# State-space stage of a fused decoder: B and C rows in rings of their own, the scan in place in SBUF, the product issued one step ahead

## The reference

```python
xn = (x - mu) * rsqrt(var + eps) * ln_w + ln_b
x_in, z = split(xn @ W_in)
xc = silu(causal_conv4(x_in) + conv_b)
dt_r, Bm, Cm = split(xc @ W_xproj)          # 8, 16 and 16 columns
dt = softplus(dt_r @ W_dt + b_dt)
def step(h, inp):                           # over the 128 tokens
    dA = exp(dt_t[:, :, None] * A)
    h = h * dA + dt_t[:, :, None] * B_t[:, None, :] * u_t[:, :, None]
    y = einsum('bdn,bn->bd', h, C_t)
y = (ys + xc * D_param) * silu(z)
out = x + y @ W_out                         # then a layer norm
```

## Time and profile before

| | us |
|---|---|
| median of 3 runs (lowest, highest) | 1881.98 (1881.71, 1882.33) |
| the profiled execution | 1878.54 |
| its span, first to last instruction | 1876.7 |
| first product of the state-space steps starts | 711.64 |
| last hC of POOL starts | 1239.76 |

### The profile page before, as it was taken

One profiled execution on the slowest core, in us unless ns is written; L12 is line 12 of the kernel. 1 busy time (PEld: TensorE's weight loads), 2 busy tenths in 40 slices (PEclk: granted clock), 3 DMA queues, 4 the chain that ended last, 5 costly groups with the idle time before them and its releaser, 6 DMA issues. The chain is left out here.

```text
span 1876.7 us, 29075 instructions
## 1 busy us (share of the span) xinstructions
PE 1478.6 (79%) x9959; PEld 992.7 (53%) x9963; DVE 1427.8 (76%) x2651; ACT 875.9 (47%) x1347; POOL 905.7 (48%) x794
## 2 busy tenths in 40 slices
PE   8989987999699986886877777658988831399991
PEld 4555545988466652332323323226767621399990
DVE  6999995879478868889888888967777757744445
ACT  3545543576544455665555645325666511022224
POOL 4446441444400116787677677654443200177653
PEclk8999998999899998998988888999999965599995
DMA  5000000000000013454444454420000050277765
GB/s 147 2 0 0 0 1 21 8 1 2 12 1 0 0 47 93 122 139 106 134 131 119 121 135 127 137 95 35 5 9 5 2 152 0 65 265 238 238 187 141
DMA packets 84090, 142.82 MB, mean 76 GB/s; under 512 B 11050, under 2 KB 36818, under 8 KB 83458
## 3 DMA queue, kind: packets, MB, share of 16 engines
q1 hardware_dynamic: 78562, 131.62, 24.1%
q0 software_dynamic: 4544, 9.32, 1.4%
q10 hardware_dynamic: 864, 0.33, 0.1%
HBM read 129.23 MB, written 12.00 MB: 75 GB/s over the span
## 5 line engine op out<-in xcount | busy, mean ns | idle before, releaser
L1552 POOL TENSOR_TENSOR m_hC<-m_h,m_BC 128x1024 f32<-128x1024 f32 x128 | 301.0, 2356 | 140.6 <-DVE m_h L1710 71.6
L1789 PE MATMUL PS<-m_hC,identf 128*128 128x512 f32 x512 | 267.7, 652 | 93.0 <-POOL m_hC L1552 93.0
L1710 DVE TENSOR_TENSOR_SCAN m_h<-m_dA,PS 128x1024 f32<-128x1024 f32 x128 | 292.6, 2286 | 4.5
L1789 PEld LDWEIGHTS PS<-m_hC,identf 128*128 128x128 f32 x512 | 98.6, 205 | 244.4 <-POOL m_hC L1552 139.6
L1669 ACT ACTIVATE m_dA<-m_DT,m_A 128x508 f32<-128x508 f32 x256 | 167.8, 711 | 118.0 <-DVE m_h L1710 105.1
L1705 DVE TENSOR_TENSOR PS<-PS,m_BC 128x1024 f32<-128x1024 f32 x128 | 157.4, 1229 | 57.1 <-DMA m_BC<-state_rows 23.5
L2243 PE MATMUL PS<-e_xT,e_WT 128*128 128x128 f32 x1136 | 139.7, 277 | 0.0
L1940 POOL DMA_INDIRECT e_XG<-token_rows,e_ids x71 | 68.9, 970 | 139.4 <-DVE e_ids L2145 118.0
L2001 ACT ACTIVATE e_Sg<-PS 128x512 f32<-128x512 f32 x71 | 42.4, 597 | 196.3 <-PE PS L2243 196.3
L2243 PEld LDWEIGHTS PS<-e_xT,e_WT 128*128 128x128 f32 x1136 | 133.7, 193 | 0.0
L2158 DVE TENSOR_TENSOR e_HT<-PS,e_Sg 128x512 f32<-128x512 f32 x71 | 49.1, 692 | 100.9 <-PE PS L2243 100.9
(11 more groups left out here) (400 smaller groups left out, 3574.3 us busy)
## 6 DMA issues: line engine op xcount, KB each, us to landing
m_BC<-state_rows SPq DMA_DIRECT2D x128, 512.0 KB, 4.7
e_WT<-in_w_wgu SPq DMA_DIRECT2D x71, 512.0 KB, 3.7
token_rows<-X SPq DMA_DIRECT2D x2, 2048.0 KB
e_Y<-expert_rows SPq DMA_DIRECT2D x16, 256.0 KB, 4.1
k_BD<-in_w_bcr SPq DMA_DIRECT2D x1, 2464.0 KB, 9.3
e_w_wd<-in_w_wd SPq DMA_DIRECT2D x1, 2048.0 KB, 8.1
out_dram<-X SPq DMA_DIRECT2D x8, 256.0 KB, 2.3
X<-in_x SPq DMA_DIRECT2D x1, 1792.0 KB, 9.0
```

Of the source, the lines that this page charges most:

```text
L1552: nc.gpsimd.tensor_tensor(hC[:, G % NY], hst[:, G % NH], wide(BC[:, G % RB, 1, :]), ALU.mult).then_inc(s["hC"], 1)
L1710: nc.vector.tensor_tensor_scan(one(hst[:, G % NH]), dA[:, G % NA].rearrange("p c b l -> p (c b l)"), one(pair(DBU)), 0.0, ALU.mult, ALU.ad ...
L1789: ins = nc.tensor.matmul(bank(YB + ch), c.identf[:, :], hC[:, G % NY, ch, :], start=False, stop=(n == NS - 1))
```

## The change

- **Rings.** B and C rows come by a transfer each, into `Bs` and `Cs`, rings of 4. A slot of `Bs` is free when the product has read it (`dBu`), one of `Cs` when POOL has (`hC`). SP issues B of step G, then C of step G - 2 (`LATE`).
- **Scan in place.** The product goes to the slot of `hst` (now a ring of 5) in SBUF, and the scan reads dA and that slot and writes the slot. Banks 3 and 4 no longer hold products.
- **One ahead.** DVE issues the product of step G + 1 before the scan of step G. It waits for B, for hC of step G - 4, and no more for a scan.
- **du in two pairs.** `IN` is banks 3 and 4 for even groups, 1 and 2 for odd ones. `staged` stands 3 steps earlier, and waits for the products of the group before last.
- **Group 0.** `corrected0` to `staged` of group 0 leave POOL and ACT; DVE computes them (`first_inputs`), the last one straight into PSUM. ACT's third piece of the logs (`c1`) is left out for it.
- Four numbers of `OWN` and the places of `store` move. The formulas of `first_inputs` are the same sum in another grouping.

```diff
-    NH, NY, NA, RB = 4, 2, 4, 4
-    IN, DBU, YB = 1, 3, 5
+    NH, NY, NA, RB = 5, 2, 4, 4
+    IN, YB = (3, 1), 5
...
-    BC = sb("BC", [P, RB, 2, T])
+    Bs, Cs = sb("Bs", [P, RB, T]), sb("Cs", [P, RB, T])
...
-           "corrected0": -11.5, "corrected1": -10.5, "softplus": -9.5, "inputs": -8.5, "z0": -11.5, "z1": -10.5, "z_copy0": -6.4, "z_copy1": -5.4,
-           "staged": 2.5, "gate": 17.5, "output0": 17.6, "output1": 18.6, "stats": 21.5, "rstd": 21.6, "norm": 26.5, "silu_z": 16.5}
+           "corrected0": -12.5, "corrected1": -11.5, "softplus": -9.5, "inputs": -7.5, "z0": -11.5, "z1": -10.5, "z_copy0": -6.4, "z_copy1": -5.4,
+           "staged": -0.5, "gate": 17.5, "output0": 17.6, "output1": 18.6, "stats": 21.5, "rstd": 21.6, "norm": 26.5, "silu_z": 16.5}
...
+    LATE = 2
+    STORE = [16] + [g * NS + 9 for g in range(1, NG - 1)]
+    LATER = ("corrected0", "corrected1", "softplus", "inputs", "staged")
...
-                sp.dma_start(BC[:, G % RB], src.to_broadcast([P, 2, T])).then_inc(bc[G % RB], 16)
+                sp.dma_start(ring[:, G % RB], src.to_broadcast([P, T])).then_inc(ready[G % RB], 16)
...
-            for G in range(NG * NS):
-                rows(G)
-                if G % NS == 12 and G // NS + 1 < NG:
-                    store(G // NS + 1)
+            for G in range(NG * NS + LATE):
+                if G < NG * NS:
+                    rows(G, 0, Bs, bs, s["dBu"])
+                if G >= LATE:
+                    rows(G - LATE, 1, Cs, cr, s["hC"])
+                if G + 1 in STORE:
+                    store(STORE.index(G + 1) + 1)
...
+                pool.wait_ge(cr[G % RB], 16 * (G // RB + 1))
                 pool.wait_ge(s["h"], G + 1)
...
-                act.wait_ge(s["du"], g + 1)
-                if g:
-                    act.wait_ge(s["dBu"], g * NS)
-                else:
-                    act.wait_ge(s["ab"], CH)
-                    act.wait_ge(before["acc0"], NG)
-                    act.wait_ge(before["acc"], NG * NR)
-                nc.scalar.copy(pair(IN), DU[:, :, :]).then_inc(s["dup"], 1)
+                act.wait_ge(s["du"], g)
+                if g >= 2:
+                    act.wait_ge(s["dBu"], (g - 1) * NS)
+                nc.scalar.copy(pair(IN[par]), DU[:, :, :]).then_inc(s["dup"], 1)
...
+            def first_inputs(g, par):
+                dve.wait_ge(s["w"], 1)
+                nc.vector.scalar_tensor_tensor(one(E1), one(E2), -1.0, one(E1), ALU.add, ALU.subtract).then_inc(s["o"], 1)
+                dve.wait_ge(s["o"], 1)
+                dve.wait_ge(s["l"], 1)
+                nc.vector.tensor_tensor(one(L), one(L), one(E1), ALU.subtract).then_inc(s["o"], 1)
+                dve.wait_ge(s["o"], 2)
+                nc.vector.tensor_tensor(one(DT[:, 0]), one(DT[:, 0]), one(L), ALU.add).then_inc(s["dt"], 1)
+                dve.wait_ge(s["dt"], 1)
+                dve.wait_ge(before["acc"], NG * NR)
+                dve.wait_ge(s["u"], CH)
+                nc.vector.tensor_tensor(pair(IN[0]), DT[:, 0], U2[:, 0], ALU.mult).then_inc(s["dup"], 1)
+
+            def product(G):
+                g, n = G // NS, G % NS
+                if n == 0:
+                    dve.wait_ge(s["dup"], g + 1)
+                dve.wait_ge(bs[G % RB], 16 * (G // RB + 1))
+                if G >= NH:
+                    dve.wait_ge(s["hC"], G - NH + 1)
+                nc.vector.tensor_tensor(hst[:, G % NH], pair(IN[g % 2]), wide(Bs[:, G % RB, :]), ALU.mult).then_inc(s["dBu"], 1)
+
             def step(g, n):
                 G = g * NS + n
-                if n == 0:
-                    dve.wait_ge(s["dup"], g + 1)
-                dve.wait_ge(bc[G % RB], 16 * (G // RB + 1))
-                if G:
-                    dve.wait_ge(s["h"], G)
-                nc.vector.tensor_tensor(pair(DBU), pair(IN), wide(BC[:, G % RB, 0, :]), ALU.mult).then_inc(s["dBu"], 1)
+                if G == 0:
+                    product(0)
+                if G + 1 < NG * NS:
+                    product(G + 1)
                 dve.wait_ge(s["dBu"], G + 1)
                 dve.wait_ge(s["dA"], G + 1)
-                if G >= NH:
-                    dve.wait_ge(s["hC"], G - NH + 1)
-                nc.vector.tensor_tensor_scan(one(hst[:, G % NH]), dA[:, G % NA].rearrange("p c b l -> p (c b l)"), one(pair(DBU)), 0.0, ALU.mult, ALU.add).then_inc(s["h"], 1)
+                nc.vector.tensor_tensor_scan(one(hst[:, G % NH]), dA[:, G % NA].rearrange("p c b l -> p (c b l)"), one(hst[:, G % NH]), 0.0, ALU.mult, ALU.add).then_inc(s["h"], 1)
```

More of the change, by code:

```diff
@@ L1401, in state_space @@
     s = c.sems("m_", "A cw wc xp0 z0 mone nm n xnp xnT xpc z zc sz u xd bcp bcs dv ab e w l c1 t dt du dup "
-                     "dA dBu h hC yacc y1 yp ng nb tw x " + LN_SEMS + " ist imv ilv irs")
-    bc = list(c.sems("m_", " ".join(f"bc{i}" for i in range(RB))).values())
+                     "dA dBu h hC o yacc y1 yp ng nb tw x " + LN_SEMS + " ist imv ilv irs")
+    bs = list(c.sems("m_", " ".join(f"bs{i}" for i in range(RB))).values())
+    cr = list(c.sems("m_", " ".join(f"cr{i}" for i in range(RB))).values())
     si = {k: s["i" + k] for k in LN_SEMS.split()}
@@ L1433, in state_space @@
     OPEN = {"inner_stats": 4, "inner_rstd": 6, "inner_norm": 7, "xn_T": 7, "xn_copy": 7, "x0": 7, "x1": 8, "x2": 8, "x3": 8, "silus": 9, "dt_b_c": 9, "parts": 10,
-            "dt0": 10, "dt1": 10, "dt_bias": 14, "exps": 16, "logs": 17, "corrected0": 17}
+            "dt0": 10, "dt1": 10, "dt_bias": 14, "exps": 16, "logs": 17}
     OWN = {"inner_stats": -28.5, "inner_rstd": -28.4, "inner_norm": -23.5, "xn_T": -25.5, "xn_copy": -19.6, "x0": -23.5, "x1": -22.5, "x2": -21.5, "x3": -20.5,
            "silus": -16.6, "dt_b_c": -18.5, "parts": -14.6, "dt0": -15.5, "dt1": -15.4, "dt_bias": -10.5, "exps": -9.5, "logs": -8.5,
-           "corrected0": -11.5, "corrected1": -10.5, "softplus": -9.5, "inputs": -8.5, "z0": -11.5, "z1": -10.5, "z_copy0": -6.4, "z_copy1": -5.4,
-           "staged": 2.5, "gate": 17.5, "output0": 17.6, "output1": 18.6, "stats": 21.5, "rstd": 21.6, "norm": 26.5, "silu_z": 16.5}
-    EARLY = {0: {"corrected1": -1, "softplus": -1, "inputs": -1, "z0": -1, "z1": 0.5, "z_copy0": 1.4, "z_copy1": 2.4, "staged": 0.5,
+           "corrected0": -12.5, "corrected1": -11.5, "softplus": -9.5, "inputs": -7.5, "z0": -11.5, "z1": -10.5, "z_copy0": -6.4, "z_copy1": -5.4,
+           "staged": -0.5, "gate": 17.5, "output0": 17.6, "output1": 18.6, "stats": 21.5, "rstd": 21.6, "norm": 26.5, "silu_z": 16.5}
+    EARLY = {0: {"first_inputs": -1, "z0": -1, "z1": 0.5, "z_copy0": 1.4, "z_copy1": 2.4,
                  "output0": 20.6, "output1": 21.6, "stats": 23.5, "rstd": 23.6, "norm": 28.5},
@@ L1461, in run @@
         for name, stage in stages.items():
-            for g in range(NG):
+            for g in range(1) if name == "first_inputs" else range(1 if name in LATER else 0, NG):
                 if g or name not in OPEN:
@@ L1481, in store, with rows @@
                 if g >= 2:
-                    sp.wait_ge(s["hC"], (g - 1) * NS)
+                    for ready in bs + cr:
+                        sp.wait_ge(ready, 16 * (g - 1) * NS // RB)
                 sp.dma_start(c.BCD[g % 2], xd[0:32, :]).then_inc(s["bcs"], 16)
-            def rows(G):
+            def rows(G, j, ring, ready, freed):
                 g, n = G // NS, G % NS
@@ L1490, in rows @@
                 if G >= RB:
-                    sp.wait_ge(s["hC"], G - RB + 1)
-                src = c.BCD[g % 2].rearrange("(o j n) t -> n o j t", o=1, n=NS)[n]
-                sp.dma_start(BC[:, G % RB], src.to_broadcast([P, 2, T])).then_inc(bc[G % RB], 16)
+                    sp.wait_ge(freed, G - RB + 1)
+                src = c.BCD[g % 2].rearrange("(o j n) t -> j n o t", o=1, n=NS)[j, n]
+                sp.dma_start(ring[:, G % RB], src.to_broadcast([P, T])).then_inc(ready[G % RB], 16)
             store(0)
-            for G in range(NG * NS):
-                rows(G)
-                if G % NS == 12 and G // NS + 1 < NG:
-                    store(G // NS + 1)
+            for G in range(NG * NS + LATE):
[5 more added lines that the diff above has]
+                    store(STORE.index(G + 1) + 1)
         @block.gpsimd
@@ L1529, in stage @@
                     if part == 0:
-                        pool.wait_ge(s["c1"], g + 1)
+                        pool.wait_ge(s["c1"], g)
                         nc.gpsimd.tensor_tensor(one(E1), one(E1), one(E2), ALU.subtract).then_inc(s["t"], 1)
                     else:
-                        pool.wait_ge(s["t"], g * 2 + 1)
+                        pool.wait_ge(s["t"], g * 2 - 1)
                         nc.gpsimd.tensor_tensor(one(L), one(L), one(E1), ALU.add).then_inc(s["t"], 1)
@@ L1537, in softplus @@
             def softplus(g, par):
-                pool.wait_ge(s["t"], g * 2 + 2)
+                pool.wait_ge(s["t"], g * 2)
```

(23 more changed lines are left out.)

## The result

The changed kernel takes 2017.6 us (median of 4 runs, 2016.1 to 2021.0) against 1881.9: a ratio of 1.073, 95% interval 1.070 to 1.077. The forecast was 2000, range 1840 to 2045. The profiled execution has a span of 2014.4 us.

The account below looks back on a forecast made before the run. DVE was taken to set the pace of the state-space steps. Exclusion +79.5, POOL's short chains +13, turns +30 and start -4 gave +118.5 on 1878.5, so 1997; plus 3.4 for the median, 2000 us, range 1840 to 2045.

Parts of the forecast that it names:

- The mechanism: State-space steps: a scan with two SBUF inputs and POOL operations reading SBUF shut each other out for the whole instruction.
- The exclusive sum: State-space stage: scans 281.6 plus POOL's tile operations 360.4, less 33.3 of hidden start-up, 608.7 against 529.2 us: +79.5.
- POOL's short chains: POOL's layer-norm chains, twice a group, 1.8 us each, in which a waiting scan may run or not: 0 to 27, taken 13.
- hand-overs: Between scans and POOL's tile operations: 256 of them, each hiding 0.13 us of start-up, -33.3 us.
- The turn of a group: The next group's first product waits for ACT's copy of du behind silus: seven turns, 0 to 42 us, taken 30.
- Rival A: The scan is left alone by POOL's reads, so the change is faster: -15 to -45 us, 1847; chance 0.27.
- exclusion: In the steps, scans and POOL's SBUF-reading operations never overlap: 2000 us, own range 1957 to 2045; chance 0.62.
- The start: Group 0's tile operations move from POOL and ACT to DVE: first scan at about 708.9 for 712.91, -4 us.
- Twice the transfers at half the size: B and C rows on SP, which has nothing else to issue: costed at nothing.
- The 0.34 us per step: DVE's step with a product issued ahead, 3.32 us for 3.66; worth nothing when scans and POOL's reads take turns.
- Rival B: The port is shared by turns, POOL at half speed beside a scan: -5 to +40 us, about 1897; chance 0.11.

Follow-up runs that it names:

- experiment 1: The changed kernel with the scan's second input from the du pair of PSUM banks, not SBUF (output not the reference's): 1864.6 us, ratio 0.9925.
- experiment 2: The kernel before with the scan's second input from a constant SBUF tile instead of the product in PSUM: 2015.2 us, ratio 1.072.
- experiment 3: The changed kernel with POOL's hC replaced by a memset that writes SBUF and reads nothing: 1870.9 us, ratio 0.994.
- experiment 6: The changed kernel with the copy of du ahead of silus on ACT (`staged` -1.7 for -0.5): 1996.2 us, ratio 1.0615.
- experiment 10: The changed kernel with the scan's second input from PSUM and the copy of du ahead of silus (`staged` -1.7): 1843.6 us, ratio 0.981.

## Why the prediction was right, and where its sizes were off

- **The mechanism** was the forecast one. The single assumption that no row showed, that a scan takes the port as a tile product does, is shown by experiments 1 and 2 from both sides: -153 and +136 us for one operand's place. Experiment 3 shows that it takes POOL's reading.
- **The exclusive sum, +79.5.** Its unit price was right (4.25 worked out, 4.29 measured in experiment 2). As a sum it was called the case without turns and chains, and the stage took more. From the first scan to the end of the last hC it was 1380.0 - 707.7 = 672.3 us, against 529.2: +143.
- **POOL's short chains, 0 to 27, taken as 13.** This is the term that was too small. I let a chain cost its own length at most. But its instructions read SBUF, and between two of them DVE may start a scan. Three per group took 2.1 to 2.2 us each, every time, and a fourth did in two groups of seven: 15.3 + 15.0 + 15.0 + 5.3 = 50.6 us for 28 instructions that need 0.2 each, so 45 us more of POOL's time. With 100 on hC and 20 on the other tile operations, POOL's work in the stage grew by 165 us (386.0 to 550.7), and its idle time fell by 22 (143.2 to 121.6): together the stage's 143. That is where POOL's time went, and not yet what each part cost, for the short instructions wait while a scan runs that had to run anyway. By the stage's own sum, 672.3 less 608.7 is 64 us, of which the turns were 21 (next point). The 43 that are left stand against the 13; no run takes the chains away alone, so it is argued, not shown, that they are the chains' and not hand-overs without a hidden start-up or PE's lower clock. In experiment 3, where POOL had time to spare, its short instructions took 43 us more too, and the stage was no longer than before (526 us).
- **The turn of a group, 30.** The waits were 48.3 us; without them 21 us went (experiment 6). The place was right, and the size was 21 where I took 30. Rival A had a turn of 28 to 56 us as well, and experiment 1 shows it without exclusion: 44.4 us of waiting. What I had not seen is that the copy's place was the best thing to mend in the kernel before.
- **The start, -4.** The first scan began at 707.67 for 712.91, so -5.2. The four L90, no longer held, took 1.12 us instead of 3.14, as forecast; but they also began 1.0 us earlier than in the execution before (699.20 for 700.19), at the end of the routed net. That leaves -4.2. One execution can't tell a microsecond here: in the kernels with `first_inputs` the first scan lies between 707.7 and 710.6.
- **Together** the span grew by 2014.4 - 1876.7 = 137.7 us, for 118.5 forecast. The turns were taken 9 too large and what stands for the chains 30 too small, so that the total came out nearer than its worst term is in part luck.
- **What was costed at nothing.** Twice the transfers at half the size: neither DVE nor POOL waits for rows in any kernel with the rings, so nothing. The 0.34 us per step are there (scan to next product 2.20, product to scan 1.12). That they are worth nothing under exclusion, no run tests by itself; it fits that experiment 2, without them, is as slow as the changed kernel. Without exclusion they brought some 8 us of 43 (experiment 10).
- **Rival A** was 1847, and experiment 1 stands for it with 1865, 15 us under the kernel before: the small end of the 15 to 45 that it was given.
- **Rival B** has no support: scans are stretched by what is left of POOL's operation, up to its whole length, and not by a constant share.

## What to carry to other kernels

Before a VectorE instruction gets a second SBUF input, look at what GpSimd does beside it: if it reads SBUF, the two run one after the other, and one operand in PSUM was worth 7% of this kernel. A short GpSimd instruction that comes just behind the start of such a scan waits for all of it, and takes ten times its length of GpSimd's time. And when a wait is removed, look for the copy or transfer that takes its place at the turn of a group: there, a single number in an order table was worth 20 us, after 4 for the rings and against some 8 for the product ahead.

## What the runs showed of the hardware that was not expected

An instruction of 4 elements per partition on POOL was held for 2 us, three times in a group, while a scan ran that had begun 0.13 us before it (903.12 and 903.25). A write-only POOL operation of 1024 elements per partition ran in 0.95 us inside a scan with two SBUF inputs, and neither felt the other (968.36 and 967.51, experiment 3).

The places of the operands cost nothing by themselves. The scan from two SBUF tiles takes 2274 ns at least, and from PSUM 2264. A tile operation of DVE that had to wait takes 1.22 or 1.23 us, whether it writes PSUM (704.12, L1716: 1.23) or SBUF (958.73: 1.22), and one that had not 1.19 to 1.20 (945.63). The mean of 1203 ns for the products of the changed kernel, against 1229 before, is this difference and not that of SBUF and PSUM.
